# Pre-norm scan and mixture of experts on one Trainium2 core: expert slots of 512 rows, raw weights split in place, mixing in two wide slots

## The chip, the cores and the metric

The kernel runs on one core of one Trainium2 chip. A core has five engines that run their own instruction streams and wait for each other on semaphores: PE (TensorE, matmuls), ACT (ScalarE), DVE (VectorE), POOL (GpSimd) and SP (SyncE, which here only starts DMAs). Engines work on SBUF (128 partitions) and on PSUM, whose eight banks hold 512 float32 values per partition each. The metric is the device time of one execution in microseconds (us); lower is better. The kernel before takes 1016.72 us (median of 3 runs, 1016.47 to 1017.0).

## The reference, cut to what matters

Input x is 4 x 1024 rows of 256 (4096 rows in all), float32. Two layers, each added to x:

```
x = x + scan_layer(layernorm(x))          # qkva projection, sigmoid gate, linear scan over time, q * y
z = layernorm(x)
logits = z @ router_w.T                   # 7 experts
top 2 of 7; top_w = softmax(top_vals)     # combine weights
expert e: down_e( silu(z @ gate_e) * (z @ up_e) )      # 256 -> 1024 -> 256
x = x + sum_k top_w[k] * expert_k(z) + shared_expert(z)
```

Each row goes through two routed experts and the shared one. The products keep nearly float32 precision: each factor is split into a rounded high part and the rest (`hi` and `lo`), and three products are summed (hi*hi, hi*lo, lo*hi).

## The kernel before, in words

The scan layer comes first, in eight groups of 512 rows. Then come slots: a slot is a set of rows of one expert. The kernel has 16 shared slots of 256 rows (10 before the routed ones, 6 after), 32 routed slots of 256 rows and 6 "lone" slots of 128 rows, which compute in plain float32. Rows of an expert are sorted in DRAM through indirect DMAs of POOL (`gather_x`); results go back in the same way (`scatter_y`), and at the end they are read (`got`), weighed by `mix_w` and added to the rows (`mix`, DVE).

One slot of 256 rows (`slot`, on each engine): PE makes gate and up for two of eight blocks of the hidden width at a time. Call such a step a unit: 24 matmuls of 256 columns, in two PSUM banks, four units in a slot. The next unit but one uses the same banks, so PE waits for `gated` of the unit two back (L1020 follows that wait). ACT takes `silu` of the gate half (L792), DVE multiplies it by the up half (L1534, `gated`), ACT rounds the product to `h_hi` (L797), DVE subtracts to get `h_lo` (L1539). Each engine runs these in order, so the next `silu` of ACT stands behind `h_hi`, which waits for DVE. After four units PE runs the down product: for each of 8 blocks and 2 tiles of 128 rows one matmul of 512 columns (L1035, `w_hi` and `w_lo` side by side) and one of 256 (L1039). Shared slots before the routed ones keep the product in SBUF (`h_early`), the others in PSUM bank 7.

Between these stand the steps for later slots. Rows of the next slot are transposed by DVE into PSUM bank 6 (`turn_x`, L1227) and split by ACT (`x_hi`, L696) and DVE (`x_lo`, L1241). Weights of an expert (gate, up, down: 1 MB each) are loaded by SP into one staging buffer `raw`; ACT rounds them in halves to `w_hi` (L753), POOL subtracts gate and down (L594) and DVE subtracts up in two halves (L1519) to get `w_lo`. Two buffers `w_both` hold split weights. PE waits for `wlo_ready` of gate and up at the start of a routed slot, and for that of down before its down product. In routed slot r, gate and up of expert slot r+2 are rounded and split during and after the down product of r, one whole slot ahead of their use; down of r+1 is rounded beside the first two units of r. The order on every engine is written out by hand; nothing reorders it.

In the first shared slots DVE also does the routing: top 2, ranks, places of the rows (`rank_...`, `places`, `find_alone`, ...), and the lists of rows by one-hot products (`hot_rows`, `hot_cols` on DVE, `list_part` on PE, eight parts).

Of the kernel before, what the change touches and what calls it, by code (L numbers as in the profile page):

```python
# [7 lines left out]
F32 = mybir.dt.float32  # L8
# [7 lines left out]
P = 128  # L16
# [6 lines left out]
def preln_scan_moe_kernel(nc, x, w_qkva, gamma, router_w, w_gate, w_up, w_down,  # L23
# [14 lines left out]
    SBN = 6  # L38
# [5 lines left out]
    FULL = ROUTED * SLOT  # L44
    THR = N // P
    COLS = NS + ROUTED * ST
    FIRST_LONE = 9
    LATE = 12
    R0 = SA + NS
    LONES = [n for n in range(FIRST_LONE, R0) if n != LATE]  # L50
    assert len(LONES) == NS and R0 % 2 == 0
    assert NS % 2 == 0 and ROUTED % 2 == 0 and COLS >= BLOCKS and (BLOCKS - E) // 2 < ROUTED
    GT = 8
    CHUNKS = TOP * TILES // GT
# [25 lines left out]
    with ExitStack() as ctx:  # L80
# [24 lines left out]
        h_hi, h_at = place("h_hi", [P, JH, SLOT], F32R)  # L105
        h_lo = sb("h_lo", [P, JH, SLOT], F32R)
        xs_hi, xs_at = place("xs_hi", [P, 2, KD, SLOT], F32R)
        xs_lo, xs_lo_at = place("xs_lo", [P, 2, KD, SLOT], F32R)
        sb("z_in_rest", [P, KD, SLOT])
# [21 lines left out]
        z_in = [sb("z_in", [P, CH // BK, KD * BK], at=xs_lo_at + 4 * KD * SLOT)] * (NC - 2) + [  # L131
# [3 lines left out]
        zT = [sb("zT", [P, KD, CH], at=xs_at)] * (TILES // CT - 3) + [  # L135
# [5 lines left out]
        owner_c = sb("owner_c", [1, ROUTED, E], at=hT_at + 8 * KD * CH + 2048)  # L141
        spill_c = sb("spill_c", [1, NS, E], at=hT_at + 8 * KD * CH + 2048 + 4 * ROUTED * EP)
        spill = sb("spill", [1, 3, EP], at=hT_at + 8 * KD * CH + 2048 + 4 * (ROUTED + NS) * EP)
        halves, odd, o_incl, o_base, lone_at, lone_to = (
            sb(n, [P, EP], at=hT_at + 12 * KD * CH + 4 * EP * i)
            for i, n in enumerate(("halves", "odd", "o_incl", "o_base", "lone_at", "lone_to")))
        spill_to = sb("spill_to", [P, 1], at=hT_at + 12 * KD * CH + 24 * EP)
# [3 lines left out]
        w_lone = [raw, w_spare[0], w_spare[1], raw, w_spare[0], w_spare[1]]  # L151
        w_first = sb("w_first", [P, 3, WPART], at=w_at[0] + 12 * WPART)
        assert len(w_lone) == NS
        xs_lone = sb("xs_lone", [P, 2, KD, SLOT], at=xs_at)
# [12 lines left out]
        got = sb("got", [P, 2, ST + 4, TOP, D], at=w_at[1])  # L167
# [27 lines left out]
        DESC, SLOTS = iota_f[:, 0:EP], iota_f[0:1, EP:EP + ROUTED]  # L195
        assert EP + ROUTED <= 48
# [9 lines left out]
        n_slots = sb("n_slots", [P, EP])  # L206
        s_incl = sb("s_incl", [P, EP])
        s_base = sb("s_base", [P, EP])
# [4 lines left out]
        owner_f = sb("owner_f", [1, NS + ROUTED])  # L213
        owner = sb("owner", [1, NS + ROUTED], I32)
# [14 lines left out]
        raw_in = [sem(f"raw_in{k}") for k in range(3)]  # L229
        lone_in = [sem(f"lone_in{i}") for i in range(NS)]  # L230
        lone_down_in = [sem(f"lone_down_in{i}") for i in range(NS)]
        first_in = [sem(f"first_in{k}") for k in range(3)]
# [57 lines left out]
        got_in = [sem("got_in0"), sem("got_in1")]  # L290
        mixed = sem("mixed")
# [1389 lines left out]
```

## Time and profile before

| | |
|---|---|
| three runs | 1016.47, 1016.72, 1017.0 us |
| profiled execution, its own time | 1016.68 us |
| its span in the trace | 1014.9 us (1.8 us lie outside it) |
| granted TensorE clock | 1.00 of full speed |
| PE / DVE / ACT / POOL busy | 98% / 62% / 52% / 49% |
| HBM read, written | 165.4 MB, 26.7 MB (189 GB/s over the span) |

Stages in the profiled execution: scan layer to 106 us, ten shared slots with routing and six lone slots to 355 us, routed slots to 908 us, six shared slots with mixing to 1011 us. A matmul's "mean ns" is its latency in the pipeline and overlaps with its neighbours; the rate at which PE works is the spacing of starts.

### The profile page before, as it was taken

The page shows a single profiled execution, that of the slowest core. Times are in us where ns is not written, and L with a number is a line of the kernel's source. Part 1 is how long each engine was busy: PE and PEld are TensorE (multiplying, and loading weights), DVE is VectorE, ACT ScalarE, POOL GpSimd, SP SyncE. Part 2 cuts the span into 40 slices and gives each one's busy share as a digit, 9 for nine tenths or more (in the row PEclk, how much of TensorE's full clock was granted, in tenths as well). Part 3 has the DMA queues.
Part 4 walks back from the last instruction along what each step waited for, and adds up shares of the span by engine and source line. Part 5 has one row for each costly group of instructions (what it writes and reads, how often), then busy time and mean ns, then how long its engine had stood idle before and what let it go on. Part 6 is the DMA issues. An engine that isn't in the chain of part 4 may idle for free.

```text
span 1014.9 us, 19709 instructions
## 1 busy us (share of the span) xinstructions
PE 998.5 (98%) x7277; PEld 941.3 (93%) x7277; DVE 629.3 (62%) x1095; ACT 523.5 (52%) x786; POOL 501.6 (49%) x282
## 2 busy tenths in 40 slices
PE   7999999999999999999999999999999999999998
PEld 6788999999999998999999999999999999999997
DVE  7997687887523365555555656565655555647876
ACT  4555433223222456666666667666666666643232
POOL 2226100000012469777777777778887777650000
PEclk9999999999999999999999999999999999999999
DMA  9333300000799748877777777777777777737441
GB/s 321 90 93 89 83 12 14 19 11 7 261 362 325 246 137 258 263 253 243 237 257 229 257 234 256 227 255 236 247 231 257 234 257 235 238 83 239 131 130 41
DMA packets 162029, 192.75 MB, mean 190 GB/s; under 512 B 76089, under 2 KB 147266, under 8 KB 151746
## 3 DMA queue, kind: packets, MB, share of 16 engines
q1 hardware_dynamic: 155248, 173.83, 53.3%
q0 software_dynamic: 6720, 18.36, 5.9%
q8 instruction: 25, 0.41, 0.2%
q14 instruction: 18, 0.15, 0.0%
q10 hardware_dynamic: 18, 0.01, 0.0%
HBM read 165.42 MB, written 26.74 MB: 189 GB/s over the span
## 4 chain that ended last, share of the span: by engine, by line
PE 88%; DVE 7%; ACT 1%; POOL 1%; DMA 1%; issue 1%; SPq 0%; DVEq 0%; POOLq 0%
PE ps L1020 51%; PE ps L1035 16%; PE ps L1039 8%; PE ps L1061 4%; PE ps L927 3%; PE ps L1069 2%; DVE y_sb L1209 2%; PE ps L911 1%; POOL w_both L594 1%; DVE hT_lo L1169 1%; ACT h_hi L797 1%; DVE h_lo L1539 1%; PE ps L938 1%; DVE h_early L1534 1%; DMA resid<-in_L_attn_x_dram 1%
## 5 line engine op out<-in xcount | busy, mean ns | idle before, releaser
L1020 PE MATMUL ps<-xs_hi,w_both 128*128 128x256 f32 x3072 | 564.7, 284 | 3.2 <-DVE ps L1534 2.4
L1020 PEld LDWEIGHTS ps<-xs_hi,w_both 128*128 128x128 f32 x3072 | 479.1, 189 | 6.0 <-DVE ps L1534 2.8
L1020 PE MATMUL ps<-xs_lo,w_both 128*128 128x256 f32 x1536 | 434.8, 283 | 0.0
L594 POOL TENSOR_TENSOR w_both<-raw,w_both 128x2048 fp32r<-128x2048 f32 x67 | 317.9, 4745 | 96.7 <-ACT w_both L753 88.4
L1020 PEld LDWEIGHTS ps<-xs_lo,w_both 128*128 128x128 f32 x1536 | 290.7, 189 | 0.1
L1035 PE MATMUL ps<-w_both,h_hi 128*128 128x512 f32 x768 | 273.5, 398 | 0.7 <-DVE h_lo L1539 0.6
L1039 PE MATMUL ps<-w_both,h_lo 128*128 128x256 f32 x768 | 215.5, 281 | 0.0
L792 ACT ACTIVATE silu<-ps 128x512 f32<-128x512 f32 x192 | 114.3, 595 | 190.5 <-PE ps L1020 190.5
L753 ACT ACTIVATE w_both<-raw 128x1024 fp32r<-128x1024 f32 x192 | 192.5, 1051 | 4.4 <-DMA raw<-in_L_ffn_w_gate_dram 2.5
L1534 DVE TENSOR_TENSOR ps<-ps,silu 128x512 f32<-128x512 f32 x160 | 111.8, 699 | 129.5 <-ACT silu L792 123.1
L1539 DVE TENSOR_TENSOR h_lo<-ps,h_hi 128x512 fp32r<-128x512 f32 x160 | 110.6, 691 | 107.8 <-ACT h_hi L797 107.8
L1035 PEld LDWEIGHTS ps<-w_both,h_hi 128*128 128x128 f32 x768 | 144.4, 188 | 34.9 <-DVE h_lo L1539 1.7
L797 ACT ACTIVATE h_hi<-ps 128x512 fp32r<-128x512 f32 x160 | 95.8, 599 | 137.2 <-DVE ps L1534 137.2
L620 POOL DMA_INDIRECT x_stage<-z_rows,idx_x x70 | 75.0, 1072 | 161.7 <-DVE idx_x L1481 134.7
L1039 PEld LDWEIGHTS ps<-w_both,h_lo 128*128 128x128 f32 x768 | 145.1, 189 | 0.0
L633 POOL DMA_INDIRECT expert_rows<-y_rows,idx_y x70 | 70.7, 1010 | 80.6 <-ACT y_rows L784 59.8
L1519 DVE TENSOR_TENSOR w_both<-raw,w_both 128x1024 fp32r<-128x1024 f32 x64 | 78.3, 1263 | 38.6 <-ACT w_both L753 38.6
L927 PE MATMUL ps<-hT_hi,wT_hi 128*128 128x512 f32 x96 | 39.8, 414 | 4.6 <-DVE hT_lo L1169 3.0
L797 ACT ACTIVATE h_hi<-h_early 128x512 fp32r<-128x512 f32 x32 | 20.2, 632 | 43.8 <-DVE h_early L1534 43.8
L927 PE MATMUL ps<-hT_hi,wT_lo 128*128 128x512 f32 x96 | 37.7, 393 | 0.0
L927 PE MATMUL ps<-hT_lo,wT_hi 128*128 128x512 f32 x96 | 37.5, 390 | 0.0
L1227 DVE STREAM_TRANSPOSE ps<-x_rows 128x256 f32<-128x256 f32 x96 | 37.3, 434 | 0.1
(191 smaller groups left out, 741.0 us busy)
## 6 DMA issues: line engine op xcount, KB each, us to landing
raw<-in_L_ffn_w_up_dram SPq DMA_DIRECT2D x33, 1024.0 KB, 5.3
raw<-in_L_ffn_w_gate_dram SPq DMA_DIRECT2D x33, 1024.0 KB, 8.5
raw<-in_L_ffn_w_down_dram SPq DMA_DIRECT2D x33, 1024.0 KB, 5.6
sorted_rows<-x_stage SPq DMA_DIRECT2D x32, 256.0 KB, 2.2
x_rows<-sorted_rows SPq DMA_DIRECT2D x128, 64.0 KB, 5.3
got<-expert_rows SPq DMA_DIRECT2D x10, 512.0 KB, 5.7
z_rows<-z_all SPq DMA_DIRECT2D x8, 512.0 KB, 2.9
x_rows<-z_rows SPq DMA_DIRECT2D x64, 64.0 KB, 2.5
```

What stands on the lines that cost most here:

```text
L594: pool.tensor_tensor(w_lo[buf][:, k, :], source[:, k, :], w_hi[buf][:, k, :].bitcast(F32), ALU.subtract).then_inc(wlo_ready[k], 1)
L620: pool.indirect_dma_start(x_stage[:, i % 2, t, :], None, z_dram, bass.IndirectOffsetOnAxis(ap=idx_x[:, c:c + 1], axis=0), bounds_check=N - ...
L753: ins = act.activation(w_hi[buf][:, k, cols], source[:, k, cols], ACT.Copy)
L792: act.activation(silu[:, par, :, :], ps[:, 2 * par:2 * par + 2, 0:SLOT], ACT.Silu).then_inc(silu_ready, 1)
L797: act.activation(h_hi[:, 2 * p:2 * p + 2, :], h32_of(par, early), ACT.Copy).then_inc(hhi_ready, 1)
L927: last = pe.matmul(ps[:, bank + e, :], w[:, part, kd, at:at + P], h[:, c, kd, :], start=i == 0, stop=i == len(terms) - 1)
L1020: last = pe.matmul(o, w[:, part, at[kd]:at[kd] + P], xx[:, u, kd, :], start=i == 0, stop=i == len(terms) - 1)
L1035: pe.matmul(ps[:, 4 + t, :].rearrange("p (b d) -> p b d", d=D), h_hi[:, j, t * P:(t + 1) * P], both[:, :, 2, j * D:(j + 1) * D], start=j = ...
L1039: last = pe.matmul(ps[:, 4 + t, 0:D], h_lo[:, j, t * P:(t + 1) * P], hi[:, 2, j * D:(j + 1) * D], start=False, stop=j == JH - 1)
L1519: ins = dve.tensor_tensor(w_lo[buf][:, k, cols], source[:, k, cols], w_hi[buf][:, k, cols].bitcast(F32), ALU.subtract)
L1534: dve.tensor_tensor(h32_of(par, early), ps[:, 2 * par:2 * par + 2, SLOT:2 * SLOT], silu[:, par, :, :], ALU.mult).then_inc(gated, 1)
L1539: dve.tensor_tensor(h_lo[:, 2 * p:2 * p + 2, :], h32_of(par, early), h_hi[:, 2 * p:2 * p + 2, :].bitcast(F32), ALU.subtract).then_inc(h_re ...
```

## The change

- **Quads.** Two slots of 256 rows of the same expert become one of 512 (`quad`). There are 7 shared quads (4 and the one among the lone slots before, 2 at the end; slots 0 and 1 stay at 256) and 12 routed quads; 8 routed slots of 256 rows ("pairs" below) follow, and the 6 lone slots stay. A unit of a quad is one hidden block: 12 matmuls of 512 columns, in two PSUM banks, eight units. `silu`, product, `h_hi` and `h_lo` of a unit have 128x512 elements as before. The down product of a quad runs its first two tiles as before (`down_wide`), then the other two as 48 matmuls of 256 columns into bank 6, so bank 6 must be free of turned rows by then.
- **Weights in place.** The staging buffer `raw` is gone; SP loads raw weights into the place of `w_lo` of the buffer where they are wanted, and POOL and DVE subtract in place. A load of gate and up can start when the slot that used this buffer is through its gate and up, and down when it is done. So an expert's weights are now rounded and split in the slot just ahead of their use. In a routed quad ACT rounds half a matrix behind `h_hi` of each of units 0 to 5 (up, gate, down); in a pair it rounds up and gate behind the four units and down after them. DVE splits up in a quad behind units 3 and 4, in a pair after unit 3; POOL splits gate, then down.
- **Rows.** A quad needs two sets of 256 rows turned: DVE turns them behind units 1 and 4 and splits them behind units 2 and 5.
- **Routing.** Three kinds of slots must be filled (quads, pairs, singles), with some more small DVE steps; the lists are made beside and after quads 2, 4 and 6.
- **Mixing.** In the two last quads ACT multiplies the fetched results by the weights (`weigh`) and DVE adds the two, then adds the sum to the rows.

The core of the diff:

```diff
-    SBN = 6
+    SBN = 4
+    QUAD = 2 * SLOT
+    QUADS = 12
+    PAIRED = ROUTED - 2 * QUADS
...
-        raw = sb("raw", [P, 3, WPART])
+        w_raw = [sb(f"w_raw{b}", [P, 3, WPART], at=w_at[b] + 12 * WPART) for b in range(2)]
...
 # POOL
-            for r in range(ROUTED):
-                if r:
-                    scatter_y(NS + r - 1)
-                split_lo(2, r + 2, 1 - r % 2)
-                if r + 3 < ROUTED:
-                    gather_x(NS + r + 3)
-                if r + 3 <= ROUTED + 1:
-                    split_lo(0, r + 3, r % 2)
+            for r in range(QUADS):
+                i = NS + 2 * r
+                gather_ahead(i + 4)
+                split_lo(0, r + 2, 1 - r % 2)
+                gather_ahead(i + 5)
+                split_lo(2, r + 2, 1 - r % 2)
+                scatter_y(i)
+                scatter_y(i + 1)
+            for r in range(QUADS, TURNS):
+                i = NS + QUADS + r
+                if i + 4 < NS + ROUTED:
+                    gather_ahead(i + 4)
+                split_lo(0, r + 2, 1 - r % 2)
+                split_lo(2, r + 2, 1 - r % 2)
+                scatter_y(i)
...
 # ACT, in a pair (slot)
+                    if nxt is not None:
+                        round_w((1, 1, 0, 0)[p], nxt[0], nxt[1], p % 2)
...
+                if nxt is not None:
+                    for half in range(2):
+                        round_w(2, nxt[0], nxt[1], half)
 # ACT, in a quad
+                    if nxt is not None and j < 6:
+                        round_w((1, 1, 0, 0, 2, 2)[j], nxt[0], nxt[1], j % 2)
...
 # PE, quad: one unit
+                    for part in range(2):
+                        terms = [(w, xx, kd) for kd in range(KD)
+                                 for w, xx in ((hi, xs_hi), (hi, xs_lo), (lo, xs_hi))]
+                        for i, (w, xx, kd) in enumerate(terms):
+                            last = pe.matmul(ps[:, 2 * (j % 2) + part, :],
+                                             w[:, part, kd * H + j * P:kd * H + (j + 1) * P],
+                                             xx[:, h // 2, kd, :], start=i == 0, stop=i == len(terms) - 1)
+                    last.then_inc(gu_psum, 1)
...
 # DVE, mixing
+                dve.tensor_tensor(sums, sums, got[:, u, p0:p1, 1, :], ALU.add).then_inc(halves_summed, len(ps_))
+                dve.wait_ge(halves_summed, MIX_FROM[j] + p1)
+                dve.tensor_tensor(rows, rows, sums, ALU.add).then_inc(mixed, len(ps_))
```

POOL in the routed slots before, one slot of its loop (`w_both_51` and `w_both_52` are the two buffers of split weights, `whi_ready0` says that gate is rounded, `whi_ready2` down):

```order
L594 TENSOR_TENSOR w_both_51<-raw,w_both_51 128x2048 [waits whi_ready2]
L620 DMA x_stage<-z_rows,idx_x 128x256 [waits x_put0,xT_psum]
L620 DMA x_stage<-z_rows,idx_x 128x256
L594 TENSOR_TENSOR w_both_52<-raw,w_both_52 128x2048 [waits whi_ready0]
L633 DMA expert_rows<-y_rows,idx_y 17152x256 [waits y_out0,down_free]
L633 DMA expert_rows<-y_rows,idx_y 17152x256
```

and now, in a pair (`w_both_50` and `w_both_51` are the two buffers now, `w_raw_98` is the raw half of the first):

```order
L642 DMA x_stage<-z_rows,idx_x 128x256 [waits x_put1,xT_psum]
L642 DMA x_stage<-z_rows,idx_x 128x256
L618 TENSOR_TENSOR w_both_50<-w_raw_98,w_both_50 128x2048 [waits whi_ready0]
L618 TENSOR_TENSOR w_both_50<-w_raw_98,w_both_50 128x2048 [waits whi_ready2]
L655 DMA expert_rows<-y_rows,idx_y 17152x256 [waits y_out0,down_free]
```

Before, gate went to one buffer and down to the other, for different slots; now both go to the same buffer, for the slot that comes next.

ACT in a routed slot before, from its third unit on:

```order
L797 ACTIVATE h_hi<-ps 128x512 [waits gated]
L696 ACTIVATE xs_hi<-ps 128x512 [waits xT_psum]
L792 ACTIVATE silu<-ps 128x512 [waits gu_psum]
L797 ACTIVATE h_hi<-ps 128x512 [waits gated]
L753 ACTIVATE w_both_52<-raw 128x1024 [waits raw_in1]
L753 ACTIVATE w_both_52<-raw 128x1024
L753 ACTIVATE w_both_52<-raw 128x1024 [waits raw_in0]
L753 ACTIVATE w_both_52<-raw 128x1024
```

and now in a pair, from the same unit:

```order
L821 ACTIVATE h_hi<-ps 128x2x256 [waits gated]
L788 ACTIVATE w_both_51<-w_raw_99 128x1024 [waits raw_in1_0]
L728 REGISTER_ALU
L729 ACTIVATE xs_hi<-ps 128x2x256 [waits xT_psum]
L816 ACTIVATE silu<-ps 128x512 [waits gu_psum]
L818 REGISTER_ALU
L821 ACTIVATE h_hi<-ps 128x2x256 [waits gated]
L788 ACTIVATE w_both_51<-w_raw_99 128x1024
L788 ACTIVATE w_both_51<-w_raw_99 128x1024 [waits raw_in1_2]
```

Gate (`raw_in0` before, `raw_in1_0` now) is now rounded between the third and fourth unit and behind the fourth, where it stood last, for a slot one further on.

DVE in a routed quad now, units 3 to 5 (before, both splits, L1519, stood after the last unit of a slot):

```order
L1706 TENSOR_TENSOR h_lo<-ps,h_hi 128x512 [waits hhi_ready]
L1660 ISA
L1661 TENSOR_TENSOR w_both_51<-w_raw_99,w_both_51 128x1024 [waits whi_ready1]
L1698 REGISTER_ALU
L1699 REGISTER_ALU [waits silu_ready]
L1700 TENSOR_TENSOR ps<-ps,silu 128x512 [waits h_ready]
L1706 TENSOR_TENSOR h_lo<-ps,h_hi 128x512 [waits hhi_ready]
L1330 STREAM_TRANSPOSE ps<-x_rows 128x256 [waits x_ld1,down_free,x_split]
L1330 STREAM_TRANSPOSE ps<-x_rows 128x256
L1661 TENSOR_TENSOR w_both_51<-w_raw_99,w_both_51 128x1024
L1698 REGISTER_ALU
L1699 REGISTER_ALU [waits silu_ready]
```

The two halves of up now stand between units, ahead of the product (L1700) of the next one.

## Rows read from the trace of the kernel before

**Rows 1.** The page, part 1: busy time of each engine, share of the span, instructions.
```profile
PE 998.5 (98%) x7277; PEld 941.3 (93%) x7277; DVE 629.3 (62%) x1095; ACT 523.5 (52%) x786; POOL 501.6 (49%) x282
```
**Rows 2.** Timeline of PE, one routed slot: start us, us, engine, line, operation.
```profile
598.82 0.28 PE L1020 MATMUL ps<-xs_hi,w_both 128*128 128x256 f32 x1
...
610.34 0.40 PE L1035 MATMUL ps<-w_both,h_hi 128*128 128x512 f32 x1
...
615.98 0.28 PE L1020 MATMUL ps<-xs_hi,w_both 128*128 128x256 f32 x1
```
**Rows 3.** Timeline of PE: starts of the first and of the third routed slot.
```profile
355.17 0.47 PE L1020 MATMUL ps<-xs_hi,w_both 128*128 128x256 f32 x1
...
392.90 0.28 PE L1020 MATMUL ps<-xs_hi,w_both 128*128 128x256 f32 x1
```
**Rows 4.** Timeline of PE, scan layer: matmuls of 512 columns, ten apart.
```profile
26.96 0.40 PE L927 MATMUL ps<-hT_lo,wT_hi 128*128 128x512 f32 x1
...
29.23 0.40 PE L927 MATMUL ps<-hT_hi,wT_lo 128*128 128x512 f32 x1
```
**Rows 5.** Timeline of ACT in the same routed slot.
```profile
601.90 0.60 ACT L792 ACTIVATE silu<-ps 128x512 f32<-128x512 f32 x1 [2.19 <-PE ps L1020]
...
604.89 0.59 ACT L792 ACTIVATE silu<-ps 128x512 f32<-128x512 f32 x1
606.34 0.60 ACT L797 ACTIVATE h_hi<-ps 128x512 fp32r<-128x512 f32 x1 [0.85 <-DVE ps L1534]
606.83 1.05 ACT L753 ACTIVATE w_both<-raw 128x1024 fp32r<-128x1024 f32 x1
607.78 0.59 ACT L792 ACTIVATE silu<-ps 128x512 f32<-128x512 f32 x1
```
**Rows 6.** Timeline of DVE in the same slot, and two rows of an earlier one.
```profile
365.26 0.78 DVE L1227 STREAM_TRANSPOSE ps<-x_rows 128x256 f32<-128x256 f32 x2
365.95 0.67 DVE L1534 TENSOR_TENSOR ps<-ps,silu 128x512 f32<-128x512 f32 x1
...
605.60 0.70 DVE L1534 TENSOR_TENSOR ps<-ps,silu 128x512 f32<-128x512 f32 x1 [0.83 <-ACT silu L792]
606.97 0.69 DVE L1539 TENSOR_TENSOR h_lo<-ps,h_hi 128x512 fp32r<-128x512 f32 x1 [0.67 <-ACT h_hi L797]
607.58 0.78 DVE L1227 STREAM_TRANSPOSE ps<-x_rows 128x256 f32<-128x256 f32 x2
...
614.52 2.36 DVE L1519 TENSOR_TENSOR w_both<-raw,w_both 128x1024 fp32r<-128x1024 f32 x2 [1.21 <-ACT w_both L753]
```
**Rows 7.** Timeline of DVE: splits of up that meet splits on POOL.
```profile
364.13 1.22 DVE L1519 TENSOR_TENSOR w_both<-raw,w_both 128x1024 fp32r<-128x1024 f32 x1
...
373.41 5.01 DVE L1519 TENSOR_TENSOR w_both<-raw,w_both 128x1024 fp32r<-128x1024 f32 x2 [2.15 <-ACT w_both L753]
```
**Rows 8.** Timeline of POOL at the same times.
```profile
364.52 5.30 POOL L594 TENSOR_TENSOR w_both<-raw,w_both 128x2048 fp32r<-128x2048 f32 x1 [5.47 <-ACT w_both L753]
371.56 4.64 POOL L594 TENSOR_TENSOR w_both<-raw,w_both 128x2048 fp32r<-128x2048 f32 x1 [1.73 <-ACT w_both L753]
```
**Rows 9.** Timeline of DVE and PE: a product, and the matmul that waited for it.
```profile
383.52 0.70 DVE L1534 TENSOR_TENSOR ps<-ps,silu 128x512 f32<-128x512 f32 x1 [2.54 <-ACT silu L792]
...
384.28 0.38 PE L1020 MATMUL ps<-xs_hi,w_both 128*128 128x256 f32 x1 [1.47 <-DVE ps L1534]
```
**Rows 10.** Timeline of DVE: routing and list steps in shared slots.
```profile
150.07 0.17 DVE L1365 TENSOR_SCALAR lone_to<-o_base 128x8 f32<-128x8 f32 x1
...
203.33 0.74 DVE L1463 TENSOR_TENSOR hot_hi<-count_f,pos_hi 128x560 f32<-128x560 f32 x1
...
205.54 0.69 DVE L1561 TENSOR_TENSOR resid<-ps,resid 128x512 f32<-128x512 f32 x1
```
**Rows 11.** DMA issues from 590 to 640 us: count, KB each, median us to landing.
```profile
raw<-in_L_ffn_w_up_dram SPq DMA_DIRECT2D x3, 1024.0 KB, 5.3
...
x_stage<-z_rows,idx_x POOLq DMA_INDIRECT x6, 5.9
```

More of the change, by code:

```diff
@@ L845, in _ @@
-            slot(NB0 - 2, 0, r=NS + ROUTED - 1, down=16 * ROUTED, gate_up=16 * ROUTED + 16)
-            slot(NB0 - 1, 1, r=NS + ROUTED, down=16 * ROUTED + 16)
-            with act.Fori(0, SBN // 2 - 1) as i:
-                for u in range(2):
-                    slot(i * 2 + (NB0 + u), u)
-            slot(NB0 + SBN - 2, 0)
-            slot(NB0 + SBN - 1, 1, last=True)
+            quad(LATE, LATE % 4, turns=())
+            lone(2, between={p: lambda p=p: round_w((1, 1, 0, 0)[p], 0, loads_of(0, 0), p % 2) for p in range(4)})
@@ L1033, in slot @@
                     for j in (2 * p, 2 * p + 1):
[L1034 to L1041 removed]
+                        last = down_wide(j, both, hi)
                     if p == 0 and down is not None:
@@ L1044, in slot, with down_wide @@
                 last.then_inc(down_psum, 1)
+            def down_wide(j, both, hi):
+                for t in range(ST):
+                    pe.matmul(ps[:, 4 + t, :].rearrange("p (b d) -> p b d", d=D),
+                              h_hi[:, j, t * P:(t + 1) * P], both[:, :, 2, j * D:(j + 1) * D],
+                              start=j == 0, stop=False)
+                    last = pe.matmul(ps[:, 4 + t, 0:D], h_lo[:, j, t * P:(t + 1) * P],
+                                     hi[:, 2, j * D:(j + 1) * D], start=False, stop=j == JH - 1)
+                return last
@@ new lines, in quad @@
+            def quad(n, h, turns=(), kind="pair", nxt=None, routed=None, shared=None, early=False, between=(), skip=NS):
+                for j in range(JH):
+                    par = j % 2
+                    gate(n, j, par, early, skip, ps[:, 2 * par + 1, :].rearrange("p (j n) -> p j n", j=2))
+                    rest(n, j, par, early, skip, h_lo[:, j, :].rearrange("p (j n) -> p j n", j=2),
+                         h_hi[:, j, :].rearrange("p (j n) -> p j n", j=2))
+                    if j in between:
+                        between[j]()
+                    for at, ahead, nth in turns:
+                        if j == at + 1 and kind == "pair":
+                            x_lo(n + ahead - skip + 1, (h + ahead) % 4)
+                    for at, ahead, nth in turns:
+                        if j == at:
+                            turn(n, h, ahead, nth, skip, kind)
+                    if nxt is not None and j in (3, 4):
+                        split_half(*nxt, j - 3)
+                if "down" in between:
+                    between["down"]()
+                if shared is not None:
+                    add_wide(n, shared * ST)
+                if "half" in between:
+                    between["half"]()
+                if shared is not None:
+                    add_narrow(n + 1, shared * ST + ST)
+                if routed is not None:
+                    dve.wait_ge(y_half, routed)
+                    dve.tensor_tensor(y_rows[:, 0, :, :], ps[:, 4:6, 0:D], y_rows[:, 0, :, :], ALU.add
@@ new lines, in _ @@
+            for i in range(4, 6):
+                lone(i)
+            with dve.Fori(0, QUADS // 2) as i:
+                for u in range(2):
+                    nth = i * (2 * LD) + loads(R0 + 2 * u + 2)
+                    quad(i * 4 + (R0 + 2 * u), 2 - 2 * u, turns=((1, 2, nth), (4, 3, nth)),
+                         nxt=(i * 2 + (u + 2), 1 - u), routed=i * 2 + (u + 1))
+            P0 = R0 + 2 * QUADS
+            with dve.Fori(0, PAIRED // 4) as i:
+                for u in range(4):
+                    slot(i * 4 + (P0 + u), (P0 + u) % 4, turns=((1, 2, i * (2 * LD) + loads(P0 + u + 2)),),
+                         nxt=(i * 4 + (QUADS + u + 2), 1 - u % 2), routed=i * 4 + (QUADS + u + 1))
```

864 lines of the change are left out of this document (481 added, 383 removed).

## The prediction

> **What bounds the kernel now.** I read the busy times first: PE is busy for 998.5 us of the span, the next engine for 629 [rows 1]. Then the timeline of PE in one routed slot: it starts gate and up at 598.82, the down product at 610.34 and the next slot at 615.98, with nothing between [rows 2]. So a slot takes 17.16 us: 96 matmuls of 256 columns in 11.52 us, 0.120 each, and 5.64 us of down. All but the first two routed slots keep this pace; those two took 392.90 - 355.17 = 37.73 us instead of 34.32 [rows 3], a wait of 3.4 us. PE's own work sets the end. The reader should next look at how late the engines behind PE run, since a longer chain there only shows once it reaches PE. In that slot ACT starts one `silu` every 2.89 us while it also rounds weights (1.45 to `h_hi`, 0.49 to the rounding, 0.95 to the next `silu`) [rows 5]: as long as PE's unit of 24 x 0.120 = 2.88. There is no reserve between them.
>
> **The change part by part**, against the profiled execution's own time, 1016.7 us (span 1014.9 and 1.8 around it; the median of the runs is 1016.7 too).
>
> *Wider matmuls.* Ten matmuls of 512 columns start over 29.23 - 26.96 = 2.27 us, 0.227 each [rows 4], against 0.240 for two of 256. A quad has 96 of them: 1.28 us less than two slots. Its last two tiles are 48 matmuls of 256 columns, 5.76 us, where it was 5.64. A quad without waits is 8 units of 2.72, 5.64 and 5.76: 33.16 us against 34.32. 19 quads: -22.0. The rows of 512 stand in the scan layer, with other operands, but the spacing exceeds the columns' share of 0.120 by the same 0.013 a matmul, so I take it whole; both ends (0.227 and 0.240) give -22 to +2.
>
> By the Trainium skill (TensorE: Matmul & The Clock Gate, Back-to-back issue gap) a sustained stream of 512-column matmuls is spaced about 131 ns; the trace says 227. With 131 a unit would take 1.57 us; the sum by that rule stands with the rivals.
>
> *Waits that go.* The first two routed slots waited for weights and DVE (3.4 us). The new kernel has the whole length of lone slots and a quad for these. -3.4; it may be 0.
>
> *A routed quad.* I follow the products (DVE, `gated`) from the start of the quad. `silu` of unit 0 starts 0.20 us behind the unit (601.90 = 598.82 + 2.88 + 0.20) and the product 0.71 behind `silu`; `h_hi` starts 0.74 after the product starts, `h_lo` 1.37, the next DVE instruction 0.61 behind `h_lo`; a turn of rows takes DVE 0.69 (365.26 to 365.95), half a split 1.18 (2.36 for two) [rows 2, 5, 6]. Product 0: 2.72 + 0.20 + 0.71 = 3.63. ACT now rounds behind each unit 0 to 5, so products 1 and 2 follow 2.89 apart: 6.52, 9.41 (a turn behind unit 1 fits in: 1.98 + 0.69). Behind unit 2 `x_hi` comes after the rounding, at 0.74 + 0.49 + 0.95 = 2.18; `x_lo` 0.63 later, as `h_lo` behind `h_hi`; the next product 0.61 later, in all 3.42: 12.83. Behind unit 3 the first half of up: 1.98 + 1.18 = 3.16: 15.99. Behind unit 4 a turn, so the second half of up wants to start at 15.99 + 1.98 + 0.69 = 18.66.
>
> Here POOL comes in. Gate is rounded at 12.83 + 0.74 + 0.49 + 1.05 = 15.11 and POOL subtracts it at once. In the trace a POOL split that began while DVE held half of up took 5.30 instead of 4.6 and ended 4.47 behind DVE's end; DVE's two halves that began beside a POOL split took 5.01 instead of 2.36 and ended 2.2 behind its end [rows 7, 8]: one stands until the other is done. So POOL ends at 16.0 + 4.5 = 20.5, the second half of up 1.1 later, and product 5 starts at 21.5. PE starts 0.76 behind the start of the product it waits for [rows 9]: unit 7 (same banks as unit 5) at 22.25 instead of 19.04. It ends at 24.97; the last `h_lo` comes in time (product 7 at 21.5 + 3.42 + 1.98 = 26.9, done at 29.0, wanted at 24.97 + 7 x 0.705 = 29.9). Quad: 24.97 + 5.64 + 5.76 = 36.4, 3.2 more than without waits. 12 of them: +38.6. Bounds: with no standing still of DVE, product 5 comes at 19.8 and the wait is 1.6 (+19); with no waits 0.
>
> What these rows show is also the rule of the Trainium skill (SBUF — State Buffer, Who interferes with whom): a DVE instruction with two SBUF inputs and a GpSimd instruction that reads SBUF share a read port, and the second blocks fully. The trace agrees, with the 5.01 us. By the opposite view (they only share bandwidth) the sum would be that of the second rival.
>
> *A pair* (8 of them). PE's unit is 2.88 again. Products at 3.79, 6.68, 9.57 and, with `x_lo`, 12.99. The second half of gate is rounded at 12.99 + 0.74 + 0.49 + 1.05 = 15.27. Only now can POOL subtract it, 4.6 us, and it is for the very next slot, which PE would start at 17.16. Before, this split was for the slot after that. DVE's two halves of up start at 12.99 + 1.98 = 14.97 and need the same port: 2.36 + 4.47 one behind the other, whoever goes first, so both are ready at 21.8, and PE starts at 21.9: +4.75, eight times (seven pairs that follow a pair, and the first quad after them): +38.0. Without the port it would be 15.3 + 4.6 + 0.2 = 20.1: +23.5. I see nothing that can hide this: PE's 5.64 us of down begin at 11.52, and the rounding is chained to the last unit.
>
> *Routing.* Small steps cost 0.2, the column half of a list part 2.2, its row half 1.2 by its 1024 elements [rows 7, 10]. In quad 2 DVE has 9.8 us of routing, turns and `x_lo` between units; a bare unit of DVE and ACT is 2.0, so the products run from 5.5 (DVE is 1.8 late from slot 1) to 29.3 and the down product waits for the last: 4.7. In quad 6 the last part of the lists is made at 33.3 and PE wants it at 30.0: 3.8 with its own lag. Quad 4: 0.9. Before, these slots lost 1. +8.5 (0 to 15).
>
> *The end.* In the last quad DVE adds 12.2 us of mixing between units: the products end at 30.2, the last `h_lo` at 32.4 against 26.7 without: +5.7. The first of the two loses 0.7 to the weighing on ACT, and one add of 0.69 less stands behind the last matmul. +5.7 (0 to 12).
>
> Lone slots and scan are the same. Sum: 1016.7 - 22.0 - 3.4 + 38.6 + 38.0 + 8.5 + 5.7 = 1082. The reduced loading (22 sets of 3 MB instead of 34 for big slots) buys nothing in this sum: PE's path through a routed slot never stood on a load [rows 2].
>
> **The rivals.**
>
> *Late weights (slower still).* SP issues up of the slot after next only behind the rows it must move: turned at 9.4, gathered by 11.9, landed 5.9 later, stored and reloaded, so issued at about 21; it lands 5.3 later [rows 11] at 26.3, and ACT wants it at 21.9 + 5.0. Margin 0.6. If DMAs queue, three us are lost in each of some quads and four pairs: 1095 to 1105. Against: the load on DMA falls by a third.
>
> *No port conflict.* Quads 34.7 and pairs 20.1: 1082 - 12 x 1.6 - 8 x 1.8 = 1048. For it: the POOL split of 371.56 kept its 4.64 while DVE's stood [rows 8], so only one side need suffer. Against: those DVE instructions had one input in PSUM.
>
> *PE stays the bound (faster than before).* If ACT or POOL get ahead so that product 5 of a quad is there by 18.3 and gate is subtracted by 17.1 in a pair, only the matmuls count: 1016.7 - 22.0 - 3.4 + 14.2 = 1005. For it: by the durations of rows 5 to 7 ACT has 18 us of work and DVE 18 in a quad of 33. Against: their order is fixed, and ACT's work lies in the first 22 us.
>
> *Matmuls much closer than 0.227* (the spacing of that page). Product 5 then comes 1.15 earlier, units and down are shorter: a routed quad 3.9 less, the others about 4: 1082 - 75 = 1007.
>
> **How the numbers follow.** Forecast 0.60, its own range 1066 to 1096 (a quad's wait uncertain by 0.8, a pair's by 0.4, routing and end by 3 each). Late weights 0.14, no conflict 0.15, PE bound 0.07, closer matmuls 0.02, the rest anywhere. The range 1042 to 1104 takes in the first three. Faster 0.08 (the last two, less their slips), within 0.2%, which is about what a measurement of this kernel can tell from no change, 0.01, slower 0.91.
>
> **What would show it.** PE waits of about 2 to 3 us inside each routed quad, released by DVE's product, the largest before unit 7; a wait of about 4.7 us at the start of each of seven pairs and the quad after them, released by POOL's gate split or DVE's up split; a DVE half split of 2.5 to 3.5 us in every routed quad; quads 36.4 apart, pairs 21.9; 512-column spacing 0.227. PE's busy time near 980 if waits count apart. I am wrong if the pairs are 17.2 apart, or if the waits of quads are released by DMAs.

## The result, and the profile after

The changed kernel takes 1114.68 us (median of 4 runs, 1112.35 to 1115.74), the kernel before 1016.86 on the same chip: 1.0958 times as long, 95% interval 1.0939 to 1.0977. Forecast were 1082 us and a range of 1042 to 1104. The direction is right, the time is 33 us too low and lies outside the range. The profiled execution took 1114.16 us (span 1112.4), and its sum is made below.

The page of the changed kernel, parts 1 and 2 (beside [rows 1]):

```profile
PE 1019.9 (92%) x5757; PEld 882.9 (79%) x5757; DVE 637.9 (57%) x1037; ACT 477.9 (43%) x778; POOL 407.6 (37%) x258
...
PEclk9999999999999999999999999999999988888899
```

ACT and POOL are busy for less time than before, DVE for 9 us more, and none of them is near the span. PE has 1520 matmuls fewer and yet is busy for 21 us more (the forecast had about 980), and its clock has a row of 8s, in tenths of full speed. What PE waited for (us in total, times, longest):

```profile
PE ps L1127 <- DVE ps L1700: 33.5, 16, 2.5
PE ps L1083 <- DVE w_both L1661: 32.0, 7, 4.6
PE ps L1127 <- DVE w_both L1661: 4.6, 1, 4.6
...
PE ps L1058 <- DVEq L1614: 2.8, 1, 2.8
```

These are the forecast waits: 2.5 inside each of the 12 routed quads, for DVE's product, and 4.6 ahead of each of seven pairs and of the quad behind them, for DVE's split of up. No DMA releases one. The timeline of PE at starts of routed quads and pairs (L1127 is a quad's unit, L1083 a pair's; beside [rows 2, 3]):

```profile
506.97 0.40 PE L1127 MATMUL ps<-xs_hi,w_both 128*128 128x512 f32 x1
...
529.21 0.50 PE L1127 MATMUL ps<-xs_hi,w_both 128*128 128x512 f32 x1 [2.49 <-DVE ps L1700]
...
543.51 0.40 PE L1127 MATMUL ps<-xs_hi,w_both 128*128 128x512 f32 x1
565.84 0.66 PE L1127 MATMUL ps<-xs_hi,w_both 128*128 128x512 f32 x1 [2.53 <-DVE ps L1700]
...
581.67 0.40 PE L1127 MATMUL ps<-xs_hi,w_both 128*128 128x512 f32 x1
...
844.85 0.28 PE L1083 MATMUL ps<-xs_hi,w_both 128*128 128x256 f32 x1
...
866.81 0.58 PE L1083 MATMUL ps<-xs_hi,w_both 128*128 128x256 f32 x1 [4.64 <-DVE w_both L1661]
...
890.09 0.43 PE L1083 MATMUL ps<-xs_hi,w_both 128*128 128x256 f32 x1 [4.55 <-DVE w_both L1661]
```

One quad takes 36.54 us (506.97 to 543.51), the next 38.16, with the same wait. Three of the twelve take 36.5 to 36.6, nine 37.8 to 38.3. The first pair takes 21.96, the next 23.28, the six behind it 23.5 to 24.0. The difference between a short and a long one stands in the table by stretches, of PE (PE busy us, granted clock, DMA share, GB/s), from 6.8 us before the second pair's first matmul, and beside the quad's wait that ends at 565.84:

```profile
860.00:866.50 6.50, 2.18 (x13) 0.99 0.38 95
867.00:869.00 2.00, 2.00 (x10) 0.50 1.01 389
869.00:871.00 2.00, 2.00 (x16) 0.80 0.99 418
871.00:873.00 2.00, 2.00 (x19) 1.00 1.00 370
...
565.80:568.00 2.20, 2.16 (x6) 0.55 0.22 60
568.00:570.00 2.00, 2.00 (x7) 0.64 0.23 66
570.00:572.00 2.00, 2.00 (x12) 1.00 0.38 131
```

The clock is at 1.00 before the wait, at half (1.2 instead of 2.4 GHz) behind it, and back at 1.00 some microseconds later. PE runs 10 matmuls in 2 us where it runs 17 at full clock, and calls that busy: this is where the busy time comes from. The same 5757 matmuls are busy for 987.9 us in the kernel below that takes 1021.7 us, with a granted clock of 1.00. The load on DMA is not the reason: its share is 1.01 in the row with 10 matmuls and 1.00 in the one with 19. Behind the wait that ends at 529.21, in the short quad, the clock stays:

```profile
529.00:531.00 2.00, 1.79 (x8) 1.00 0.21 66
```

The sum against the forecast, from starts of PE: up to the first routed quad 392.79 instead of 355.2 + 34.3 for two more slots - 5.8 for five wider quads + 8.5 = 392.2 (+0.6); twelve routed quads 452.1 instead of 436.8 (+15.3); eight pairs 187.8 instead of 175.2 (+12.6); the first quad of the end 36.1 instead of 33.9 (+2.2); the last 39.3 instead of 38.9 (+0.4). That is 31.1 of 32.2.

### The profile page after: what moved, and what is told of

The parts are those of the page before. It is cut to its first block, busy times and chain, and to the rows that moved or that the text cites. A ratio compares the mean times of both kernels' runs of the same rounds, so it can differ in the third digit from the quotient of the medians.

```text
span 1112.4 us, 16252 instructions
## 1 busy us (share of the span) xinstructions
PE 1019.9 (92%) x5757; PEld 882.9 (79%) x5757; DVE 637.9 (57%) x1037; ACT 477.9 (43%) x778; POOL 407.6 (37%) x258
## 4 chain that ended last, share of the span: by engine, by line
PE 49%; DVE 23%; ACT 15%; issue 10%; DVEq 0%; DMA 0%; POOL 0%; SPq 0%; ACTq 0%
PE ps L1127 16%; PE ps L1146 9%; DVE ps L1700 7%; DVE w_both L1661 6%; PE ps L1105 5%; PE ps L1083 5%; PE ps L1166 4%; ACT w_both L788 4%; ACT h_hi L849 3%; PE ps L990 3%; ACT silu L844 3%; PE ps L1108 3%; PE ps L1174 2%; ACT silu L816 2%; DVE y_sb L1312 2%
## 5 line engine op out<-in xcount | busy, mean ns | idle before, releaser
L1127 PE MATMUL ps<-xs_hi,w_both 128*128 128x512 f32 x1216 | 402.8, 405 | 41.4 <-DVE ps L1700 33.5
L1127 PEld LDWEIGHTS ps<-xs_hi,w_both 128*128 128x128 f32 x1216 | 236.2, 194 | 108.1 <-DVE ps L1700 49.6
L618 POOL TENSOR_TENSOR w_both<-w_raw,w_both 128x2048 fp32r<-128x2048 f32 x45 | 227.3, 5058 | 95.0 <-ACT w_both L788 86.3
L1127 PE MATMUL ps<-xs_lo,w_both 128*128 128x512 f32 x608 | 243.4, 400 | 0.0
L1700 DVE TENSOR_TENSOR ps<-ps,silu 128x512 f32<-128x512 f32 x160 | 111.3, 696 | 191.8 <-ACT silu L844 135.4
L1105 PE MATMUL ps<-w_both,h_hi 128*128 128x512 f32 x464 | 165.5, 399 | 1.8 <-DVE h_lo L1706 1.8
L1083 PE MATMUL ps<-xs_hi,w_both 128*128 128x256 f32 x640 | 130.1, 303 | 32.8 <-DVE w_both L1661 32.0
L1083 PEld LDWEIGHTS ps<-xs_hi,w_both 128*128 128x128 f32 x640 | 110.6, 210 | 35.5 <-issue 35.4
L1127 PEld LDWEIGHTS ps<-xs_lo,w_both 128*128 128x128 f32 x608 | 118.5, 195 | 22.8
L788 ACT ACTIVATE w_both<-w_raw 128x1024 fp32r<-128x1024 f32 x126 | 130.8, 1051 | 0.0
L1146 PE MATMUL ps<-w_both,h_hi 128*128 128x256 f32 x608 | 111.6, 286 | 0.0
L1105 PEld LDWEIGHTS ps<-w_both,h_hi 128*128 128x128 f32 x464 | 87.3, 188 | 23.5 <-DVE h_lo L1706 3.0
L1083 PE MATMUL ps<-xs_lo,w_both 128*128 128x256 f32 x320 | 96.2, 301 | 0.0
```

What stands on the lines that cost most here:

```text
L618: pool.tensor_tensor(w_lo[buf][:, k, :], w_raw[buf][:, k, :], w_hi[buf][:, k, :].bitcast(F32), ALU.subtract).then_inc(wlo_ready[k], 1)
L788: ins = act.activation(w_hi[buf][:, k, cols], w_raw[buf][:, k, cols], ACT.Copy)
L1083: last = pe.matmul(o, w[:, part, at[kd]:at[kd] + P], unit(xx, h)[:, kd, :], start=i == 0, stop=i == len(terms) - 1)
L1105: pe.matmul(ps[:, 4 + t, :].rearrange("p (b d) -> p b d", d=D), h_hi[:, j, t * P:(t + 1) * P], both[:, :, 2, j * D:(j + 1) * D], start=j = ...
L1127: last = pe.matmul(ps[:, 2 * (j % 2) + part, :], w[:, part, kd * H + j * P:kd * H + (j + 1) * P], xx[:, h // 2, kd, :], start=i == 0, stop ...
L1146: last = pe.matmul(ps[:, 6, (t - ST) * D:(t - ST + 1) * D], a[:, j, t * P:(t + 1) * P], w[:, 2, j * D:(j + 1) * D], start=j == 0 and i == ...
```

## The experiments

Each kernel is the changed one with the edit that is shown. Times are medians; the ratio is to the kernel before, with its 95% interval.

**Is the clock the cause, or only a sign?** Matmuls whose results are overwritten fill the waits, and nothing else is changed.

```diff
+def fill(bank, x, count):
+    for _ in range(count):
+        pe.matmul(ps[:, bank, :], x[:, 0, 0:P], x[:, 0, :], start=True, stop=True)
 # slot, at its start: 36 of 256 columns; quad behind the pairs: fill(0, ..., 19)
 # routed quad, ahead of unit 7
+                        pe.wait_ge(down_free, n + 1)
+                        fill(4, xs_hi[:, h // 2], 10)
```

> The changed kernel with extra matmuls whose results are overwritten, placed where PE stands in its waits: 36 of 256 columns at the start of each pair, 19 of 512 at the start of the quad behind the pairs, 10 of 512 ahead of unit 7 of each routed quad. They need only what is there already, and the waits themselves stay. Theory A: the time beyond the forecast is TensorE's granted clock, which the trace of the changed kernel shows at 0.50 for some 3.4 us behind most of these waits (5 to 7 us in the later pairs). Then the granted clock stays at 1.00, routed quads are 36.5 apart instead of 37.7 on average, pairs 21.9 instead of 23.7; the first pair had no wait and pays its 4.3 us of filling: 1114.7 - 13.8 - 12.2 - 2 + 4.3 = about 1091. Rival B: the clock only follows from the waits and costs nothing, the chain through ACT, DVE and POOL sets the pace. Then 1115 to 1120.

Measured: 1089.99 us, 1.0723 (1.0705 to 1.0741). The granted clock over the whole span is 0.999 instead of 0.965. The stretches of PE in this kernel, around the second pair's start at 856.77 and behind it:

```profile
860.00:866.50 6.50, 6.50 (x57) 1.00 0.83 308
867.00:869.00 2.00, 2.00 (x17) 1.00 0.10 20
```

Its routed quads are 36.49 to 36.82 apart, its pairs 21.9 each, with the wait still there beneath the filling. The first pair pays for its filling (the quad ahead of it and the filling 40.86 instead of 36.55). So 24.7 us are gained, 29 without those 4.3. In the traces the routed quads give 13.2 of it, the pairs 12.5 and the quad behind them 1.5, in all 27.2; the other 1.2 lie in quad 6, whose wait is not filled and behind which this trace shows no half clock (more on that below). Quads, pairs and the quad behind them exceeded the forecast by 30.1. So the clock is 27 us of that, and the rest is the forecast's own sizes: with the clock at 1.00 the twelve quads take 438.9 and not 436.8, and the quad behind the pairs 34.6 and not 33.9. Rival B, by which the chain through the other engines sets this part too, would have had 1115. This settles the cause of the miss. The Trainium skill (TensorE: Matmul & The Clock Gate, HAM oscillation — how this bites in real kernels) tells of a matmul kernel in which PE waits for data in every step and restarts on the halved clock each time. The trace agrees, with 0.50 behind the 4.64; and here waits of 2.5 did it in nine quads of twelve.

**Is it POOL that holds DVE up in the quads?** Only the order on POOL is changed.

```diff
                 gather_ahead(i + 4)
-                split_lo(0, r + 2, 1 - r % 2)
                 gather_ahead(i + 5)
+                split_lo(0, r + 2, 1 - r % 2)
                 split_lo(2, r + 2, 1 - r % 2)
```

> POOL in the routed quads: both gathers of rows are issued ahead of the gate split, nothing else. Theory A: the second half of DVE's split of up stands still because POOL subtracts gate at that time (DVE's half takes 2.56 us on average over all, 3.5 to 4 us where it is blocked). With the gathers in front, gate's split starts 1.5 to 2 us later, the first half and most of the second half of DVE are through, the wait ahead of unit 7 shrinks from 2.5 to about 1 and the half clock behind it goes where the wait is short: quads 34.8 to 36 apart, 1085 to 1100. Rival B: only who waits changes, the gate split then blocks the second half all the same: quads 37.7, 1115 as before.

Measured: 1081.29 us, 1.0635 (1.0617 to 1.0653). The timeline of DVE of the changed kernel at the second half of up, with POOL's gate split behind it, and then those of this one:

```profile
525.57 2.98 DVE L1661 TENSOR_TENSOR w_both<-w_raw,w_both 128x1024 fp32r<-128x1024 f32 x1
528.47 0.69 DVE L1700 TENSOR_TENSOR ps<-ps,silu 128x512 f32<-128x512 f32 x1
...
522.18 5.28 POOL L618 TENSOR_TENSOR w_both<-w_raw,w_both 128x2048 fp32r<-128x2048 f32 x1 [2.71 <-ACT w_both L788]
```

```profile
514.63 1.20 DVE L1661 TENSOR_TENSOR w_both<-w_raw,w_both 128x1024 fp32r<-128x1024 f32 x1
515.75 0.69 DVE L1700 TENSOR_TENSOR ps<-ps,silu 128x512 f32<-128x512 f32 x1
...
518.06 4.62 POOL L618 TENSOR_TENSOR w_both<-w_raw,w_both 128x2048 fp32r<-128x2048 f32 x1
```

In the changed kernel the half split took 2.98 and ended 1.1 behind POOL's end (522.18 + 5.28 = 527.46); it takes 1.20 when POOL comes later. PE's wait falls from 2.5 to 0.75, quads are 34.7 to 35.0 apart, and none shows a half clock. In the traces the twelve quads take 417.5 us instead of 452.1: of these 34.6, 12 x 1.75 = 21 are the wait and the other 13.6 the clock. Theory A holds, and the time is 4 us below its range, since no quad has a half clock any more. The pairs are as they were. This is the forecast's lower bound for a quad, "with no standing still of DVE": product 5 at 19.8 us and 1.6 lost in all. Product 5 starts at 19.72 (515.75 - 496.03), and the quads lose 34.8 - 33.2 = 1.6, 0.75 of it ahead of unit 7.

**And with DVE's split out of the chain?**

```diff
-                    if nxt is not None and j in (3, 4):
-                        split_half(*nxt, j - 3)
+                if nxt is not None:
+                    split_up(*nxt)
```

> In the routed quads DVE splits up behind unit 7 instead of one half behind each of units 3 and 4. Theory A: product 5 is then late for no reason that is left; the wait ahead of unit 7 goes and with it the half clock behind it; the split is done by about 29 us of the quad's 33.2. Routed quads 33.2 to 34 apart instead of 37.7: 1114.7 - 12 x 4.1 = 1065 (1060 to 1072). Rival B: the split at the end comes too late for the next quad's start because POOL's down split holds the port: a wait of 1 to 3 us at the start of each quad in place of the one inside, 1085 to 1115.

Measured: 1067.95 us, 1.0498 (1.048 to 1.0515). Quads are 33.62 to 33.94 apart, 0.5 above the 33.2 of bare matmuls, in steps of 0.13 to 0.17 ahead of units 6 and 7 and of the down product. Theory A holds. So 12 quads lost 47 us for two DVE instructions of 1.2 us each that stood in the chain of products instead of behind it. The pairs, which this edit does not touch, take 190.4 us in the trace instead of 187.8, with the same waits of 4.5 to 4.7: what the clock takes behind one and the same wait is not a fixed sum.

**The pairs: is it the order of rounding?**

```diff
-                        round_w((1, 1, 0, 0)[p], nxt[0], nxt[1], p % 2)
+                        round_w((0, 0, 1, 1)[p], nxt[0], nxt[1], p % 2)
 # SP: gate ahead of up, and both ahead of put_and_load
```

> Only in the pairs: ACT rounds gate ahead of up, so that POOL can subtract gate while the last units run, and SP loads gate first and ahead of the moves of rows. Theory A: the pair's wait is the chain gate rounded last, POOL 4.6 us, DVE blocked beside it. With gate rounded behind units 0 and 1, POOL is through by about 14 us and DVE's up follows its last product unblocked: pairs 17.5 to 19 apart instead of 23.7 (with the half clock gone), the half clock behind them goes: 1114.7 - 8 x 5.2 = about 1073 (1066 to 1082). Rival B: the loads are late, since gate's raw rows arrive only when the previous use of the buffer is over: the wait stays above 3 us, released by a DMA through ACT, 1095 to 1112.

Measured: 1099.98 us, 1.082 (1.0802 to 1.0838). This is a miss of 27 us. The time lies in rival B's range, but the cause is neither theory's: the waits, now of 6.7 to 6.8 us, are released by DVE's split of up, and the next run shows that the loads are in time. The first four intervals became longer, 24.2, 26.3, 26.7 and 25.5 us, then 20.3 and three of 18.06. The timeline of DVE in a long one and in a short one, then the rounding of the second half of gate on ACT in the long one, and then POOL in both:

```profile
885.35 8.45 DVE L1661 TENSOR_TENSOR w_both<-w_raw,w_both 128x1024 fp32r<-128x1024 f32 x2 [0.33 <-ACT w_both L788]
...
963.89 2.36 DVE L1661 TENSOR_TENSOR w_both<-w_raw,w_both 128x1024 fp32r<-128x1024 f32 x2 [0.32 <-ACT w_both L788]
```

```profile
877.91 1.05 ACT L788 ACTIVATE w_both<-w_raw 128x1024 fp32r<-128x1024 f32 x1
```

```profile
880.23 1.06 POOL L642 DMA_INDIRECT x_stage<-z_rows,idx_x  x1 [8.92 <-DVE ps L1330]
881.59 1.03 POOL L642 DMA_INDIRECT x_stage<-z_rows,idx_x  x1 [0.30 <-issue]
882.65 4.63 POOL L618 TENSOR_TENSOR w_both<-w_raw,w_both 128x2048 fp32r<-128x2048 f32 x1
887.24 5.48 POOL L618 TENSOR_TENSOR w_both<-w_raw,w_both 128x2048 fp32r<-128x2048 f32 x1
...
957.59 4.62 POOL L618 TENSOR_TENSOR w_both<-w_raw,w_both 128x2048 fp32r<-128x2048 f32 x1 [7.86 <-ACT w_both L788]
965.76 4.97 POOL L618 TENSOR_TENSOR w_both<-w_raw,w_both 128x2048 fp32r<-128x2048 f32 x1 [3.55 <-ACT w_both L788]
```

In the pairs with gathers POOL sits at a gather until DVE has turned the rows of that slot (8.92 idle). Gate is rounded at 877.91 + 1.05 = 878.96, but its split begins only behind the two gathers, at 882.65, and that of down follows without a gap. So both meet DVE's split of up, whose two halves take 8.45 instead of 2.36. One by one the halves are:

```profile
885.35 3.02 DVE L1661 TENSOR_TENSOR w_both<-w_raw,w_both 128x1024 fp32r<-128x1024 f32 x1 [0.33 <-ACT w_both L788]
888.29 5.51 DVE L1661 TENSOR_TENSOR w_both<-w_raw,w_both 128x1024 fp32r<-128x1024 f32 x1
```

The first ends 1.1 behind POOL's gate split (887.28), which is its own length, and the split of down, which started at 887.24, takes 5.48 for 4.63. The second half then ends 1.1 behind that one (892.72). The two engines take turns: each half of up waits for one split of POOL. I had forgotten POOL's queue: what stands ahead of the split on its engine. The last pairs, which gather nothing, show what the order is worth.

**Gate ahead of the gathers.** The two edits above (up behind the units in quads, gate first in pairs) and one on POOL.

```diff
+                split_lo(0, r + 2, 1 - r % 2)
                 if i + 4 < NS + ROUTED:
                     gather_ahead(i + 4)
-                split_lo(0, r + 2, 1 - r % 2)
                 split_lo(2, r + 2, 1 - r % 2)
```

> Three changes of order: DVE splits up behind unit 7 in the quads (as in the run on that alone, 1067.95, which is the kernel to compare with), gate is rounded ahead of up and loaded first in the pairs (as in the run on that alone), and POOL in a pair subtracts gate ahead of the two gathers of rows. Theory: in the run with gate first, the five pairs with gathers became longer (24 to 26.7 us) and the four without became 18.06, because there POOL sat at a gather until 854 and then subtracted gate and down in one piece (10.1 us), and DVE's split of up stood still through both (8.45 us). With gate ahead of the gathers all eight pairs take 18.1 instead of 24: 1068 - 8 x 5.9 - 2 = 1019 (1015 to 1024). Rival: the gathers are not the cause, but the loads are (the later pairs move no rows, so their DMAs come sooner): the first four pairs stay at 22 us and more, 1035 to 1045.

Measured: 1021.7 us, 1.0051 (1.0036 to 1.0067). All eight pairs take 18.04 to 18.15, with their row moves; the loads were not the reason. (The expectation counts five long pairs; the trace has four and one of 20.3. And DVE did not stand still through both of POOL's splits at a stretch: it had its turn between them, as the rows above show.) Of the chain only DVE's two halves are left, behind the last rounding, and PE waits for them for 0.6 to 0.7:

```profile
850.31 0.38 PE L1083 MATMUL ps<-xs_hi,w_both 128*128 128x256 f32 x1 [0.62 <-DVE w_both L1661]
```

```profile
865.76 2.36 DVE L1661 TENSOR_TENSOR w_both<-w_raw,w_both 128x1024 fp32r<-128x1024 f32 x2 [0.33 <-ACT w_both L788]
```

**The two ends alone.** The routing and mixing terms, priced on the changed kernel. As built, it adds two of the fetched tiles of the second group to the rows of others (the first form of all orders below does so too); the right version makes these additions in two steps of two tiles instead of one of four.

```diff
-... JH: [6, 7]}
+... JH: [6], JH + 1: [7]}      # part 7 of the lists behind tile 2 of the down product
-                "half": lambda: mix(1, range(0, 2))})
+                "half": lambda: mix(1, range(0, 4)), "end": lambda: mix(1, range(4, 8))})
# last quad: 4 tiles of the second group behind unit 1, of the third 2 behind 3, 2 behind 4, 4 behind 5
```

> The changed kernel with only two of those edits: the last part of the lists behind tile 2 in quad 6, and the mixing moved into DVE's idle time at the end of the first quad of mixing. It prices the two outer terms of the forecast (routing 8.5, of which 3.8 in quad 6, and the end 5.7) by themselves. Theory: 1114.7 - 4.2 - 5.3 = 1105 (1103 to 1107). Rival: the waits there are covered by others or by the clock, and it stays above 1110.

Measured: 1108.49 us, 1.0906 (1.0889 to 1.0922): 6.2 of the 9.5 expected. PE's wait for the lists (2.8) is gone, but a wait of 1.14 appears in the next quad, since DVE's small steps behind the lists now reach into it. In the last quad PE's waits are four of 0.4 and one of 1.28, where they were 1.11, 0.41, 1.41, 0.42 and 1.24. In the traces the stretch up to the first routed quad is 2.4 shorter and that from the last quad on 2.3, so the two ends are worth 4.7. The rest comes from quads and pairs that this edit does not touch: in this trace five of the twelve routed quads kept the clock instead of three. The next two runs show what limits the last quad.

**All orders together, first form.** Beside the edits above, in a pair the first half of up has a signal of its own, so DVE subtracts it earlier.

```diff
+                    dve.wait_ge(up_half, halves)
+                    split_half(*nxt, 0, wait=False)
+                    dve.wait_ge(whi_ready[1], nxt[0] + 1)
+                    split_half(*nxt, 1)
-                    split_up(*nxt)
```

> The kernel with both orders (that of the run beside it) with three more changes of order. In a pair DVE subtracts the first half of up as soon as that half is rounded (a signal of its own), so up is ready at 17.3 instead of 18.0: pairs 17.2 to 17.4, -5 to -6. In quad 6 the last part of the lists is made behind tile 2 of the down product instead of ahead of it: the wait of 2.8 and the half clock behind it go, -4. At the end DVE mixes 8 of the 12 tiles of the second group in its idle time at the end of the first of the two quads, and only three times 4 tiles between units of the last: that quad 34 instead of 39.3, -5.3. Theory: the new layout without waits is worth what its wider matmuls save, 1019 - 15 = about 1004 (999 to 1010), faster than the kernel before (1016.9). Rival: something else gives way (DVE's h_lo late in a pair, rows of the first lone slots late behind the later lists, the second quad's first unit late behind the mixing), 1010 to 1020.

Measured: 1013.27 us, 0.9969 (0.9957 to 0.9981); 9 us more than expected, in the rival's range. Pairs take 17.64, not 17.3, which is 2.7 in all, and the last quad 37.6, not 34; the wait of 1.14 behind quad 6 is here too. In the last quad ACT is the limit, which I had not counted. Its timeline there, behind one unit:

```profile
988.19 0.60 ACT L852 ACTIVATE h_hi<-ps 128x512 fp32r<-128x512 f32 x1 [0.77 <-DVE ps L1705]
988.68 1.70 ACT L907 ACTIVATE got<-got,mix_w 128x256 f32<-128x256 f32 x4
990.29 0.58 ACT L847 ACTIVATE silu<-ps 128x512 f32<-128x512 f32 x1
...
991.63 0.60 ACT L852 ACTIVATE h_hi<-ps 128x512 fp32r<-128x512 f32 x1 [0.77 <-DVE ps L1705]
```

From `h_hi` to `h_hi` it needs 3.44 us with two tiles weighed between, where PE's unit is 2.72. This also corrects the forecast's term for the end, which laid the delay on DVE's adds alone. Where DVE adds four tiles as well, it is 4.43 (991.63 to 996.06).

**The mixing spread out.**

```diff
-                j: lambda j=j: weigh(2, range(2 * j - 2, 2 * j)) for j in range(1, 7)})
+                j: lambda j=j: weigh(2, range(j - 1, j)) for j in range(1, 8)})
 # DVE: 2 tiles behind each of units 0 and 1, one behind each of units 2 to 7, 6 behind the last;
# tiles 0 to 3 of the second group in two steps, so that they go to their own rows
```

> The kernel with all orders changed (1013.27), with the mixing of the last quad arranged anew: there ScalarE weighs 2 tiles (1.7 us) behind each of six units, which makes its step 3.44 instead of PE's 2.72, and VectorE adds 4 tiles (2.44 us) behind three of them. Now ScalarE weighs one tile (0.8) behind each unit from 1 on and the rest behind the last unit, and VectorE adds one tile behind each unit from 2 on. Theory A: what is late in the last quad is these two engines' added work between units; the quad ends 2 to 4 us sooner, 1009.5 to 1011.5. Rival B: the fetched tiles or the last adds set the end, 1012 to 1014.

Measured: 1012.45 us, 0.9953 (0.9939 to 0.9967), so 4.7 us faster than the kernel before. The 0.8 us that part it from the first form are not clear of noise: the intervals of the two ratios overlap. PE has no wait left in the last quad; it goes from 970.59 to 1004.2, 33.6 us, instead of 37.6. But the span ends 6.4 us behind PE, not 3.9: DVE stands 1.71 for the last weighed tiles and adds PE's last result late. So both are partly right: in the traces the quad gained 4.0 and the last adds took back 2.5. This execution also came to the last quad 0.7 later, with a granted clock of 0.72 from 12 to 18 us, in the scan layer, where the first form has 1.00. The expected 1009.5 to 1011.5 is missed by 1, and the time lies in rival B's range.

```profile
1000.89 1.23 DVE L1653 TENSOR_TENSOR got<-got 128x1024 f32<-128x1024 f32 x1 [1.71 <-ACT got L907]
...
1006.46 0.69 DVE L1697 TENSOR_TENSOR resid<-ps,resid 128x512 f32<-128x512 f32 x1
```

## Why the prediction was right in its steps and wrong in its time

- *Wider matmuls, 0.227 each.* Right. The last shared quad ahead of the lone slots has no waits and takes 33.19 (forecast 33.16); the spacing in it is 0.227. The rival of closer matmuls falls.
- *Waits that go, -3.4.* Right: the first routed quad has no wait at its start.
- *A routed quad, 36.4, with 3.2 of waiting.* The chain is right. In the quad of 506.97 product 5 starts at 21.50 (forecast 21.5) and unit 7 at 22.24 (22.25), and the DVE half stands still for POOL. Where the clock stays, the quad takes 36.5. The mean is 37.67.
- *A pair, 21.9, released by the split of up.* Right for the first (21.96) and for all eight with the waits filled (21.9). The mean is 23.5.
- *Late weights.* No wait is released by a DMA; that rival falls, as does the one of PE as the bound. Its 1095 to 1105 was nearer to the measured time than my 1082, but its mechanism is not in the trace.
- *No port conflict.* Falls for DVE: 2.98 instead of 1.20 beside POOL's split, and 5.55 in the pairs.
- *Routing, +8.5.* 9.1 by the start of the first routed quad. Of this 1.4 is half clock behind the wait in quad 6: the run with POOL's other order kept the clock there and starts the first routed quad at 391.44 instead of 392.79. Quad 6 takes 41.62 us; 37.24 with the later list part.
- *The end, +5.7.* About right in size (39.3 for 38.9), with ACT as a second limit beside DVE.

The step that failed is the pricing of a wait. The forecast wrote the quad as "24.97 + 5.64 + 5.76 = 36.4, 3.2 more than without waits" and the pair as "+4.75, eight times": it took PE's rate behind a wait to be its rate before it. The clock behind it is half for a while, and that cost 1.3 to 1.8 us in nine quads of twelve, 1.4 to 2.1 in seven pairs and 1.5 in the quad behind them. Twenty waits of 2.5 to 4.6 us were worth some 27 us more than their length, and a range made of uncertain waits, with the clock held, could not take it in. The profile of before could not show it: the 3.4 us of its first two routed slots [rows 3] are short waits, the longest of them 1.47 us [rows 9], and the clock behind that one is 1.00:

```profile
384.00:386.00 2.00, 1.72 (x14) 1.00 0.44 150
```

A clock of 1.00 was the figure of a kernel without long waits, and I carried it over to one with twenty, without a term or a rival for it.

Open stays why three of the twelve equal waits in the quads kept the clock. It is not the place in the loop: with the same twelve waits of 2.5, five quads kept it in the run with gate rounded first and five in the run on the two ends. And the wait of 2.8 in quad 6 is the same in six kernels; three of their traces show the half clock behind it and three do not. This is PE behind that wait in the changed kernel, and then in the one with POOL's other order:

```profile
255.50:258.50 3.00, 3.00 (x18) 0.50 0.01 3
```

```profile
255.50:258.50 3.00, 3.00 (x30) 1.00 0.01 3
```

So what follows a wait of 2.5 to 2.8 us differs by 1.3 us and more between cases that look alike here, and a difference of 2 or 3 us between two kernels with many such waits tells little. The price of weighing on ScalarE against VectorE's old single step was not tried by itself.

## What to carry to other kernels

A wait of PE of 2.5 us and more cost here its length and, mostly, a slower clock behind it (waits of 0.6 to 0.75 us in the quads and pairs did not), so price waits with both, and see in the granted clock, stretch by stretch, what the matmuls behind each wait ran at. When the sum of a planned change has some twenty new waits of 2 us and more, first look for the one instruction in the chain that could stand behind it: here two DVE subtractions moved behind the units gave 47 us, and one POOL split moved ahead of two gathers, with gate rounded first, another 46. Look on each engine for what is queued ahead of the instruction that you count on, not only for when its inputs are ready.

## What was not expected of the hardware

- Twelve waits of 2.49 to 2.53 us, at the same place of a loop: behind nine the clock was at half, behind three it was not. With waits of 0.75 there, no quad of the twelve was longer than 35.04. Behind every one of the eight waits of 4.5 to 4.6 the time that followed was longer than with the waits filled.
- A DVE subtraction with both inputs in SBUF took 2.98 for 1.20 beside one on POOL, and ended 1.1 behind POOL's end. Beside two on POOL that follow each other without a gap, two of DVE took 8.45 for 2.36: the first ran between the two of POOL, whose second took 5.48 for 4.63, and the second waited for that one (the same in all four long pairs, within 0.03). The Trainium skill (SBUF — State Buffer, Who interferes with whom) has the exclusive lock, and the trace agrees; that the engine that waits gets the next turn, though the other has its next instruction ready, is what this trace adds.
